# Mamba scan and mixture of experts in one kernel: C by DMA and h in PSUM from step 28, experts from step 28, a denser chain per batch

## The reference

```python
# block 1: layer norm, 4 chunks of 32 channels per image, d_inner 64, 16 states
xi, z = split(x @ in_proj); xc = silu(causal_conv4(xi) + conv_b)
dt, B, C = split(xc @ x_proj); dt = softplus(dt @ dt_proj + dt_b); A = -exp(A_log)
h[t] = exp(dt[t] * A) * h[t-1] + dt[t] * xc[t] * B[t]        # for each of 16 states s
y[t] = sum_s h[t, s] * C[t, s] + D * xc[t]
ym = (y * silu(z)) @ out_proj + skip * chunk
x = x + layer_norm(ym) @ proj_w.T + proj_b
# block 2: t = layer_norm(x); 16 experts of width 256, all computed for all tokens
logits = t @ router.T; two largest, softmax of the two -> combine[token, expert]
out = x + sum_e combine[:, e] * ((silu(t @ Wg[e]) * (t @ Wu[e])) @ Wd[e])
```

## Time and profile before

| | |
|---|---|
| median of 3 runs | 328.65 us (327.45 to 331.87) |
| profiled execution | 329.45 us, span of the profile 327.6 us |
| busy in the span | PE 286.3 us (87%), DVE 244.3 (75%), POOL 179.2 (55%), ACT 151.8 (46%) |
| chain that ended last | PE 35%, issue 22%, POOL 15%, DVE 4% |
| DMA | 33.64 MB, mean 103 GB/s |

### The profile page before, as it was taken

How to read it: one execution, slowest core, us unless ns; L and a number is a source line. 1 busy time by engine, 2 the same in 40 slices (tenths; PEclk the granted TensorE clock), 3 DMA queues, 4 the chain that set the end, 5 groups by cost and what they waited for, 6 DMA issues and landing times.

```text
span 327.6 us, 3741 instructions
## 1 busy us (share of the span) xinstructions
PE 286.3 (87%) x1120; PEld 199.0 (61%) x1120; DVE 244.3 (75%) x366; ACT 151.8 (46%) x220; POOL 179.2 (55%) x184
## 2 busy tenths in 40 slices
PE   7987397877984798999888899988999999999996
PEld 6734122223431266676566576765688888888885
DVE  2499989999697378898977989797884565555553
ACT  3679546541551334765433365743426363222231
POOL 4001659986357173888799688878861214331310
PEclk9999879996998799999999999999999999999999
DMA  7913975443241330433223423430111111221110
GB/s 261 348 35 107 254 210 168 148 139 127 79 136 57 120 128 33 120 105 96 96 94 125 123 80 114 122 89 19 66 48 44 54 32 34 72 74 58 41 32 18
DMA packets 21621, 33.64 MB, mean 103 GB/s; under 512 B 2848, under 2 KB 8032, under 8 KB 21600
## 3 DMA queue, kind: packets, MB, share of 16 engines
q1 hardware_dynamic: 16720, 24.39, 24.0%
q10 hardware_dynamic: 4880, 9.00, 8.9%
HBM read 32.53 MB, written 0.85 MB: 102 GB/s over the span
## 4 chain that ended last, share of the span: by engine, by line
PE 35%; issue 22%; POOL 15%; DVE 4%; POOLq 0%; DVEq 0%
PE bank L853 10%; PE bank L868 10%; PE bank L835 9%; POOL xs L316 6%; POOL y L292 5%; PE bank L712 4%; POOL ring L286 3%; DVE ring L608 2%; DVE ring L619 2%; POOL chk L304 1%; PE bank L789 0%; PE bank L788 0%; DVE zs L672 0%; POOL w L300 0%; DVE X L676 0%
## 5 line engine op out<-in xcount | busy, mean ns | idle before, releaser
L485 ACT ACTIVATE dt<-bank,cst 128x512 f32<-128x512 f32 x64 | 44.0, 687 | 112.4 <-PE bank L835 112.3
L286 POOL TENSOR_TENSOR ring<-dtx,ring 128x512 f32<-128x512 f32 x64 | 81.0, 1277 | 18.2 <-DVE ring L608 11.4
L608 DVE TENSOR_TENSOR_SCAN ring<-bank,ring 128x512 f32<-128x512 f32 x64 | 77.6, 1213 | 7.1 <-issue 6.7
L853 PE MATMUL bank<-xs,Wu 128*128 128x256 f32 x256 | 68.0, 388 | 10.3 <-POOL xs L316 5.6
L316 POOL TENSOR_TENSOR xs<-xm,Gs 128x512 f32<-128x512 f32 x32 | 41.4, 1294 | 59.1 <-DMA Gs<-CE_far 54.9
L662 DVE SCALAR_TENSOR_TENSOR dt<-dt,bank 128x512 f32<-128x512 f32 x64 | 43.6, 682 | 36.5 <-ACT dt L485 36.5
L835 PE MATMUL bank<-xm,Wg 128*128 128x256 f32 x256 | 65.7, 379 | 0.0
L434 ACT ACTIVATE bank<-dt,cst,A 128x510 f32<-128x510 f32 x64 | 49.7, 777 | 30.4 <-DVE ring L608 28.0
L853 PEld LDWEIGHTS bank<-xs,Wu 128*128 128x128 f32 x256 | 46.3, 190 | 22.6 <-issue 13.0
L835 PEld LDWEIGHTS bank<-xm,Wg 128*128 128x128 f32 x256 | 48.6, 190 | 7.0 <-issue 0.5
L619 DVE TENSOR_TENSOR ring<-ring,bank 128x512 f32<-128x512 f32 x62 | 41.6, 671 | 14.9 <-PE bank L712 14.6
(11 more groups left out here) (108 smaller groups left out, 229.7 us busy)
## 6 DMA issues: line engine op xcount, KB each, us to landing
ring<-B_far SPq DMA_DIRECT2D x128, 128.0 KB, 3.0
Gs<-CE_far ACTq DMA_DIRECT2D x32, 256.0 KB, 3.3
Wg<-gate_w SPq DMA_DIRECT2D x1, 2048.0 KB, 10.3
Wu<-up_w SPq DMA_DIRECT2D x1, 2048.0 KB, 15.7
par<-params ACTq DMA_DIRECT2D x1, 533.5 KB, 4.2
X<-x SPq DMA_DIRECT2D x2, 256.0 KB, 4.5
out<-X SPq DMA_DIRECT2D x4, 128.0 KB, 2.2
B_far<-B_rows SPq DMA_DIRECT2D x4, 64.0 KB, 2.6
```

The lines of the kernel that those rows point to most:

```text
L286: g.tensor_tensor(u[:, k % 3], dtx[:, k // NS, :], Bs[:, k % B_RING], ALU.mult).then_inc(S["u_r"], 1)
L485: a.activation(th[n % 2], bank[gate_bank(n)][:], ACT.Tanh, scale=0.5, bias=zero).then_inc(S["th_r"], 1)
L608: v.tensor_tensor_scan(h[:, k % 3], bank[da_bank(k)][:], u[:, k % 3], 0.0, ALU.mult, ALU.add)\
L853: o = t.matmul(bank[up_bank(n)][:, f * T:(f + 1) * T], Wu[:, e, f * P:(f + 1) * P], xs[:, pr % 2, ts], start=True, stop=True)
```

## The change

- `FIRST` becomes 28: items begin beside step 28, slot n holds step 28 + n, 36 slots hold both an item and a step, 28 hold an item alone.
- From step 28 C is no longer spread by PE. SP's two DMAs for a step bring B and C (4 KB per partition in place of 2 KB), the ring has 6 places and a place comes free with `weigh`. `scan` writes h to PSUM bank 7 from step 28, and `weigh(k)` (SBUF C times PSUM h) comes in the same slot as `scan(k)`, behind `hidden(n)`. Rings of u and of the weighed states have 4 places.
- D x enters the sum of states by a PE matmul with diag(D) (`skip_D`). For batches 2 and 3 the last state and POOL's running sum are added by PE ("total"). DVE's `finish_group` of two operations becomes one ("gated").
- The chain has new parts and slots. "centre" makes proj and mean subtraction in one accumulation; the residual x is made later ("x1", PE and ACT). The mixing weights are made by DVE in 5 small operations ("mix", and two comparisons in "top") and no longer by POOL. The first part is in slot 0 or 1, the gates are written in slot 8 or 9 and spread from slot 10; of batch b's next items the first is in slot 12 (before: slot 16). In a slot PE's part now comes behind `up(n)` and ahead of `down(n-2)` and `gate(n+1)`; on DVE in the steps alone ahead of `weigh(k-1)`.
- Start: Wd is loaded right behind Wu and ahead of all rows; 6 steps of B are spread ahead (before 4); the rows of batches 2 and 3 are copied by ACT (`bc_rows`), their C no longer goes to PE. A small matmul (`keep_warm(1, 7)`) is added to every step alone below 26.
- In the prologue: two more matmuls, two more small DVE operations, one more on POOL, and 128 more columns of parameters.

```diff
 STEPS = BATCH * NS
-FIRST = 2 * NS
+FIRST = 28
 ITEMS = BATCH * E
...
-BESIDE_STEPS = {"DVE": {1: 0, 5: 5, 6: 7, 9: 12, 10: 14, 12: 16},
-                "POOL": {12: 16},
-                "PE": {2: 1, 3: 3, 5: 6, 6: 8, 7: 10, 9: 13, 13: 17},
-                "ACT": {3: 2, 4: 4, 7: 9, 8: 11, 10: 15, 13: 18}}
-BESIDE_ITEMS = {"DVE": {1: 0, 4: 5, 5: 7, 8: 12, 9: 14, 11: 16},
-                "POOL": {11: 16},
-                "PE": {2: 1, 3: 3, 5: 6, 6: 8, 7: 10, 9: 13, 12: 17},
-                "ACT": {2: 2, 3: 4, 6: 9, 7: 11, 10: 15, 12: 18}}
+BESIDE_STEPS = {"DVE": {1: "gated", 4: "norm", 6: "tokens", 7: "top", 8: "mix"},
+                "PE": {1: "out", 2: "var", 4: "centre", 5: "var_t", 7: "logits", 8: "turn", 9: "x1"},
+                "ACT": {1: "sq", 2: "rstd", 4: "sq_t", 5: "rstd_t", 7: "exp", 8: "gates", 9: "x1", 10: "spread"}}
+BESIDE_ITEMS = {"DVE": {0: "gated", 3: "norm", 6: "tokens", 7: "top", 8: "mix"},
+                "PE": {0: "total", 1: "out", 2: "var", 4: "centre", 5: "var_t", 7: "logits", 9: "turn", 10: "x1",
+                       11: "skip_D"},
+                "ACT": {1: "sq", 2: "rstd", 4: "sq_t", 5: "rstd_t", 8: "exp", 9: "gates", 10: "x1"}}
...
-        R = 4
-        STATE_SUM = (5, 6)
+        R, H = 4, 7
+        STATE_SUM = (5, 6, 6, 6)
...
         def sum_bank(b):
-            return 6 if b < BATCH - 1 else 3
+            return 3 if b < BATCH - 1 else 7
...
+        def by_pe(k):
+            return k < BY_PE or k % NS == NS - 1
+        def red_count(k):
+            return sum(1 for i in range(k) if by_pe(i))
         def acc_count(k):
-            return sum(1 for i in range(FIRST, k) if i % NS)
...
-            def spread_b(k):
+            sp.dma_start(Wd[:], down_w.rearrange("e (f p) h -> p e f h", p=P)).then_inc(S["wd_in"], 16)
+            def spread_bc(k):
                 b, s = divmod(k, NS)
                 if s == 0:
                     sp.wait_ge(S[f"far{b}"], 16)
-                if k >= B_RING:
-                    sp.wait_ge(S["u_r"], k - B_RING + 1)
+                old = k - BC_RING
+                if old >= 0:
+                    sp.wait_ge(S["u_r" if old < FIRST else "hc_r"], old + 1)
+                width = N if k < FIRST else 2 * N
+                row = BC_far[b].rearrange("(j s w) n -> j s (w n)", w=2, j=2)[:, s:s + 1]
                 for j in range(2):
-                    sp.dma_start(Bs[DI * j:DI * (j + 1), k % B_RING, :],
-                                 B_far[b, NS * j + s:NS * j + s + 1, :].broadcast_to([DI, N]))\
-                        .then_inc(S[f"Bs_in{k % B_RING}"], 16)
+                    sp.dma_start(BCs[DI * j:DI * (j + 1), k % BC_RING].rearrange("p w n -> p (w n)")[:, 0:width],
+                                 row[j, :, 0:width].broadcast_to([DI, width])).then_inc(S[f"BC_in{k % BC_RING}"], 16)
...
             put_rows(0)
-            for k in range(B_RING):
-                spread_b(k)
-            sp.dma_start(Wd[:], down_w.rearrange("e (f p) h -> p e f h", p=P)).then_inc(S["wd_in"], 16)
+            for k in range(BC_RING):
+                spread_bc(k)
             put_rows(1)
-            for k in range(B_RING, STEPS):
-                spread_b(k)
+            for k in range(BC_RING, STEPS):
+                spread_bc(k)
...
+            scan_input(1)
             for k in range(FIRST):
-                scan_input(k + 1)
+                scan_input(k + 2)
...
             for n in range(ITEMS):
                 k = step_at(n)
-                if k + 1 < STEPS:
-                    scan_input(k + 1)
+                if k + 2 < STEPS:
+                    scan_input(k + 2)
+                add_state(k - 1)
...
-                if k <= STEPS:
-                    add_state(k - 1)
-                back(*chain("POOL", k))
...
+            def bc_rows(b):
+                act.wait_ge(S["bc_r"], b + 1)
+                a.activation(BC_rows[:, b, :], bank[b][0:4 * NS, :], ACT.Copy).then_inc(S["brow_a"], 1)
...
+            def back(item, b, tables):
+                if item == "sq":
+                    act.wait_ge(S["op_r"], b + 1)
+                    a.activation(sq[:, b, :], bank[R][:, 0:T], ACT.Square, bias=zero).then_inc(S["bsq_r"], 1)
...
+                if item == "exp":
+                    for i in range(BLK):
+                        act.wait_ge(S["top_r"], BLK * b + i + 1)
+                        a.activation(e1[:, i, :], top[:, i, 0:1], ACT.Exp, scale=-1.0, bias=top[:, i, 1:2])\
+                            .then_inc(S["ex_r"], 1)
+                    act.wait_ge(S["ex_r"], BLK * (b + 1))
+                    a.activation(e_sum[:], e1[:], ACT.Copy, bias=1.0).then_inc(S["sum_r"], 1)
+                if item == "gates":
+                    act.wait_ge(S["tr_r"], BLK * (b + 1))
+                    a.activation(CE[:, b, :], bank[R][0:E, 0:T], ACT.Copy, scale=0.5).then_inc(S["ceh_r"], 1)
+                    act.wait_ge(S["ceh_r"], b + 1)
+                    act.dma_start(CE_far[b].rearrange("g (e t) -> (g e) t", t=T), CE[:, b, :])\
+                        .then_inc(S[f"ce_far{b}"], 16)
+                if item == "x1":
+                    act.wait_ge(S["x1p_r"], b + 1)
+                    act.wait_ge(S["bias_r"], 1)
+                    a.activation(X[:, b, :], bank[R][:, T:2 * T], ACT.Identity, bias=bias[:]).then_inc(S["x1_r"], 1)
+                if item == "spread":
+                    spread_gate(0)
+                    spread_gate(1)
...
+                back(*chain("ACT", k), True)
+                if n % E == E - 2 and n + 2 < ITEMS:
+                    spread_gate(n // 2 + 1)
                 pr = n // 2 + 2
                 if n % 2 == 0 and pr < ITEMS // 2 and 2 * pr % E:
                     spread_gate(pr)
-                if n % E == E - 3 and n + 3 < ITEMS:
-                    spread_gate((n + 3) // 2)
-                back(*chain("ACT", k), True)
...
             def scan(k):
...
-                if k >= 3:
-                    dve.wait_ge(S["hc_r"], k - 2)
-                v.tensor_tensor_scan(h[:, k % 3], bank[da_bank(k)][:], u[:, k % 3], 0.0, ALU.mult, ALU.add)\
+                if k > FIRST:
+                    dve.wait_ge(S["hc_r"], k)
+                elif k >= H_RING:
+                    dve.wait_ge(S["hc_r"], k - H_RING + 1)
+                dst = h[:, k % H_RING] if k < FIRST else bank[H][:]
+                v.tensor_tensor_scan(dst, bank[da_bank(k)][:], u[:, k % U_RING], 0.0, ALU.mult, ALU.add)\
...
             def weigh(k):
-                dve.wait_ge(S["pC"], k + 1)
                 dve.wait_ge(S["scan_r"], k + 1)
...
-                dst = y[:, k // NS, :] if k >= FIRST and k % NS == 0 else hc[:, k % 3]
-                v.tensor_tensor(dst, h[:, k % 3], bank[c_bank(k)][:], ALU.mult).then_inc(S["hc_r"], 1)
-            def finish_group(b):
-                if b < 2:
-                    dve.wait_ge(S["red_r"], NS * (b + 1))
-                    total = bank[STATE_SUM[b]][:]
+                old = k - HC_RING
+                if old >= 0 and by_pe(old):
+                    dve.wait_ge(S["red_r"], red_count(old + 1))
+                elif old >= 0 and old % NS:
+                    dve.wait_ge(S["acc_r"], acc_count(old + 1))
+                dst = y[:, k // NS, :] if k >= BY_PE and k % NS == 0 else hc[:, k % HC_RING]
+                if k < FIRST:
+                    dve.wait_ge(S["pC"], k + 1)
+                    v.tensor_tensor(dst, h[:, k % H_RING], bank[c_bank(k)][:], ALU.mult).then_inc(S["hc_r"], 1)
                 else:
-                    dve.wait_ge(S["acc_r"], acc_count(NS * (b + 1)))
-                    total = y[:, b, :]
-                v.scalar_tensor_tensor(y[:, b, :], xc[:, b, :], p("D"), total, ALU.mult, ALU.add)\
-                    .then_inc(S["yg_r"], 1)
-                dve.wait_ge(S["yg_r"], b + 1)
-                v.tensor_tensor(y[:, b, :], y[:, b, :], zs[:, b, :], ALU.mult).then_inc(S["y_r"], 1)
...
+            def back(item, b):
+                if item == "gated":
+                    if b < BY_PE // NS:
+                        dve.wait_ge(S["red_r"], NS * (b + 1))
+                    else:
+                        dve.wait_ge(S["tot_r"], b - BY_PE // NS + 1)
+                    v.tensor_tensor(y[:, b, :], zs[:, b, :], bank[STATE_SUM[b]][:], ALU.mult).then_inc(S["y_r"], 1)
...
+                    dve.wait_ge(S["topi_r"], BLK * (b + 1))
+                    v.tensor_copy(topf, topi[:, :, 0:2]).then_inc(S["topf_r"], 1)
+                    dve.wait_ge(S["topf_r"], b + 1)
+                    for j in range(2):
+                        v.tensor_tensor(oh[:, j], iota_e[:], topf[:, :, j:j + 1].broadcast_to([P, BLK, E]),
+                                        ALU.is_equal).then_inc(S["eq_r"], 1)
...
                     dve.wait_ge(S["sum_r"], b + 1)
-                    v.reciprocal(w01[:, :, 0:1], w01[:, :, 0:1]).then_inc(S["w0_r"], 1)
+                    v.reciprocal(w01[:, :, 0:1], e_sum[:]).then_inc(S["w0_r"], 1)
```

(73 more changed lines are left out.)

276 lines of the change are left out of this document (126 added, 150 removed).

## The result

The changed kernel takes 335.6 us (median of 20 runs, 330.8 to 337.8), the kernel before 329.2 beside it (327.2 to 331.9, and one run of 694.4). The ratio is 1.0139, 95% interval 1.0103 to 1.0174. It is slower, clear of the noise, but by less than the 2% that I counted as no change. I had said 330.5, in a range of 318 to 339. The profiled execution takes 334.86 us, span 333.1: 5.4 more than its counterpart, where my sum said 1.7 more.

What follows compares the result with a forecast made beforehand. Waits between engines were taken to set the pace in the middle stages, PE in the last. Terms -15.6 + 19.0 - 1.7 = +1.7 us gave 330.4 from the 328.65 median, stated as 330.5 us; 8-in-10 range 318 to 339.

Steps and rivals of the forecast that it cites:

- The start: Prologue up to scan 0: added operations lie under ACT's tables and roots, costing 0, at most 0.3 us.
- Steps 0 to 16: First steps alone: POOL's wait for B goes, 3.0 us saved; step 16 begins at 66.5 instead of 69.54.
- Steps 16 to gate 0: Steps 16 to 27 with batch 0's chain: 31.1 us together, DVE's gate(0) at 97.6.
- rival 3: PE's clock stays low in batch 0's chain: +3.3, 334 us; chance 0.11 together with rival 4.
- 36 shared slots: Slots with step and item: 143.2 us against 124.2; 111.6 at 3.1 a slot, sums 2.2, chains 14.0 and 15.4.
- first items: Batch starts in shared slots: gates spread late in slot 10, up of the new batch 3.1 late, 2.7 us stays.
- sums of states 27 to 31: PE carries these sums in five shared slots, +0.45 us each, 2.2 us.
- The tail: 28 items alone: 72.5 + 7.3 + 8.7 = 88.5 us, 1.7 shorter than before.
- The unknowns: Costs without rows: scan writing PSUM 0, bounds -0.1 and +0.1 per slot; 4 KB row transfers 0.
- Rival 1: Faster: PE's chain parts stay hidden in shared slots and tail, 13.4 us less, 317 us; chance 0.28.
- Rival 2: Slower: doubled spread delays gates, landing after 6.0 not 3.3 us at three batch starts, +8.1, 338.6 us; chance 0.15.
- Rival 4: The freed C buys nothing, POOL holds 3.2 a slot: +3.6, 334 us; chance 0.11 together with rival 3.

Runs made afterwards that it cites:

- e1: Changed kernel with PE's chain parts moved to the end of the slot, behind the next item's gate matmuls: 324.3 us, 0.9859 of before.
- e8: Changed kernel with the scan's h in an SBUF ring from step 28 on, not in PSUM: 336.4 us, 1.0245 of before.
- e4: Changed kernel with ten of the first filling matmuls in place of eight: 332.6 us, 1.0132 of before.
- e6: e5 plus gates copied and CE_far issued ahead of the tanh, first Gs one slot earlier, ten filling matmuls for eight: 315.9 us, 0.9579 of before.
- e7: e6 with items begun at step 32 in place of 28: 319.9 us, 0.9698 of before.
- e10: e6 without the Ln and the two table loads around it in chains beside items (output not the reference's): 310.2 us, 0.9449 of before.
- e11: e6 with two filling matmuls in place of one in each of steps 16 to 25: 317.3 us, 0.9636 of before.
- e2: Changed kernel with the first Gs of a batch issued by ACT ahead of the tanh and decay: 332.6 us, 1.0133 of before.
- e3: Changed kernel with items begun at step 32 in place of 28: 334.7 us, 1.0186 of before.
- e5: e1 with the logits and the turn (transpose) again between up and down matmuls, other PE parts last: 326.8 us, 0.9927 of before.
- e12: Kernel before the change with only PE's chain parts moved between an item's up and down matmuls: 352.0 us, 1.0704 of before.
- e9: Kernel before the change with ten of the first filling matmuls in place of eight: 329.1 us, 1.0000 of before.

## Why the prediction was right, and where it was off

The total was in the range and on the right side of 2%, 5.1 us above the forecast by the medians, 3.3 by the ratio (1.0139 of 329.2 is 333.8). Against its own execution the forecast was +1.7 and the change +5.4; the steps are off by +3.1, -0.2, +2.3, -1.6 and +0.2.

**The start (0 to 0.3 forecast, 3.1 measured): wrong.** I priced the added operations and not PE's clock. Of the 3.1 us, 1.8 are the four passes over X and 0.2 their later start (5.51 for 5.30). In the seven kernels whose passes took 1.95 to 2.36 us (e1, e8, e4, e6, e7, e10, e11) scan 0 stands at 35.7 to 36.3, and 0.5 us is left in each when passes and start are taken off: that is the added work, which I had put at 0 to 0.3. The last 0.6 in the changed kernel is open; its clock entry comes at 10.4 us, in e2, e3 and e5 at 9.2 to 9.5. With eight filling matmuls the passes took 3.67 to 3.75 us in five profiles (the changed kernel, e2, e3, e5, e12) and 1.95 in three (before, e1, e8). Which of them a kernel gets is not settled.

**Steps 0 to 16 (31.5 forecast, 31.3 measured): right**, with no wait of POOL for B and step 6 at 49.9, 11.8 behind scan 0 (11.5 worked out).

**Steps 16 to gate 0 (31.1, measured 33.4): short by 2.3.** Part of it is what rival 3 named: PE at the lower clock from 92.5 to 95.5 us, inside the chain of batch 0, and DVE standing 2.7 us for the first tanh. Kernels with half clock there from about 88 to 95 us (e4, e6, e10) take 34.6 to 34.8 us for this stage, those with half of that (the changed kernel, e1, e2, e5, e8) 33.4, so I estimate 1.3 us for what the changed kernel had and leave 1 open. More filling does not cure it (e11).

```profile
92.50:95.50 3.00, 3.00 (x8) 1.50 (x7) 2.97 (x6) 1.60 (x3) 1.81 (x2) 0.50 0.11 22
```

**36 shared slots (143.2, measured 141.6): right for the parts of a chain, not for the first items.** The ten slots without a long part take 31.4 us, 3.14 each (3.1 forecast). Forecast and measured beyond 3.1, in order from total: total 2.0 and 1.65; out 0.7 and 1.1 (0.8 in batch 2); var 1.2 and 1.2; root 1.9 and 1.9; centre 0 and -0.1; var_t 0.5 and 0.55; root 1.8 and 1.9; top 1.1 and 1.15; mix 1.2 and 0.95; turn 0.1 and -0.1 (1.6 in batch 2, where PE's passes fell to half clock); x1 1.5 and 1.5; skip_D 0.5 and 0.35. The first item of batch 1 took 3.7 beyond (PE waits 2.70 us, then `down` and `gate` take 1.47 and 1.91 at half clock) and that of batch 2 1.0 (a wait of 1.21), where 2.7 was said for each: the sum is near, 4.7 for 5.4, each size is not. The 2.2 us for the sums of states 27 to 31 were hardly paid: they lie where PE idles. So it is in part luck that the stage is only 1.6 off: sums not paid stand against half clocks not forecast. e1 shows that the place between `up` and `gate` causes the excess of out and x1 and half of var's, e10 that 1.65 us of each root's slot are the table loads and the Ln, e2 and e6 that the batch start is the late issue of Gs; CE_far, whose landing can hold that issue, was taken at 1.4 us.

**The tail (88.5, measured 88.7): right**, and e1 shows 3.7 us of it to be the place of PE's parts.

**The unknowns.** The scan into PSUM takes 1229 ns against 1217: +0.01 a slot, inside my bounds of 0.1. What I did not ask is what the other place would cost: e8 has it, 0.3 us an operation.

**The rivals.** Rival 1 fell: the parts do not stay hidden. (Of the 14.6 us that it leaned on the earlier trace rows, which are of the whole run, only 9.5 lie in the shared slots.) The kernel with the parts and the gates placed otherwise, 315.9, comes near where that rival stood (317), but not by its sum: gate 0 is 4.4 us later and the shared stage 6.7 shorter (128.9 for 135.6). Rival 2 fell as it was put: the first pairs landed in 3.1 to 4.1 us, not 6.0, and none in the changed kernel took over 4.8. A relative of it is there: CE_far, 16 KB, landed in 1.4 us in all twelve cases of the three kernels with small rows (before, e9, e12), and in up to 4.7 us in those with double rows. No run separates the rows from the other edits. The rule that the rival leaned on (the Trainium skill, DMA: Bandwidth & Descriptors, Issuing engines are not separate DMA queues) agrees with that in kind. Rival 3 held in part. Rival 4 fell: two quiet slots take 2.92, and the ten 3.14 on average.

## What to carry to other kernels

Before moving an instruction forward in an in-order queue, ask what it waits for in that slot and who stands behind it. A part that still waits belongs behind everything that others need (e1: var, out and x1). For one that has its input, here the logits and the turn, neither place is shown to be better: e1 and e5 take the same time from gate 0 on, and e6 with all of PE's parts last was not run. What begins a long latency, here copy and spread of the gates for the next batch, goes ahead of the engine's routine work: that and two filling matmuls are all that separates e6 from e5, 10.9 us. Before explaining a slot that grew by who waits for whom, compare the durations of PE's passes in it: several of these slots grew by PE's half clock alone. And when a stage is shortened, look for the next place where its end meets something issued at a fixed slot.

## What the runs showed of the hardware that was not expected

- A wait of PE can cost twice. Behind the waits of 3.23 us in e5 and 3.54 us in e12, the next two groups of four passes took 2.08 and 1.70, 1.92 and 1.91 us where they take 1.03; the granted clock there is 0.50, its lower level (1.2 of 2.4 GHz): 1.7 and 1.8 us on top of the wait. In the changed kernel the slot of item 29 (turn) is 4.69 us for that reason (clock 0.50 from 219 to 222), that of item 13 3.01. Not every such wait does it: after 2.50 us before `up(48)` of the changed kernel and 2.53 before `up(16)` of e1 the groups behind took 1.03 again.
- Ten filling matmuls in place of eight, so that PE stands at most 0.5 us before X, gave passes of 1.95 to 2.36 us in all six kernels that had them. With eight, the idle time does not tell which it will be: 1.95 us came behind 0.72, 0.96 and 1.20 us of it, 3.67 to 3.75 behind 0.63 to 0.95. The Trainium skill, TensorE: Matmul & The Clock Gate, What's actually happening, says that the number of matmuls at the lower clock differs from run to run of one kernel. The eight profiles are of eight kernels, one run each, so they can only agree in kind; of one kernel there are the 20 runs of the changed one, whose fastest (330.8 us) had a mean granted clock of 0.984 where the others had 0.959 to 0.979.
- DVE's product with both factors in SBUF took 964 ns and with one in PSUM 674, with POOL's product at work beside it (1374 and 1272 ns). The Trainium skill, SBUF — State Buffer, SBUF: two separate sides, says that DVE operations with two inputs in SBUF and GpSimd operations that read SBUF shut each other out; the rows agree in kind.
- A DMA share of 0.30 raised to 0.55 moved the median landing of the gates in the shared slots from 3.8 to 3.9 us only, but single landings more: CE_far, 16 KB and 1.4 us before, took 3.8 us once in the changed kernel and 3.7 in e2, and the second pair of batch 1 took 6.5 us in e1 and e2.
